# First attention of an eight-layer kernel: the order of extra product and transposes in TensorE's units

## The reference, cut to what matters

```
q = rope((x @ Wq.T + bq)) * key_weight / sqrt(64)   # 32 heads of 64
k = rope(x @ Wk.T + bk)                             # 8 key heads of 64
v = x @ Wv.T + bv                                   # 8 value heads of 64
p = softmax(causal(q @ k.T))                        # per head, 256 x 256
x = x + (concat(p @ v) @ Wo.T + bo)
```

## Time and profile before

| | us |
|---|---|
| median of 3 runs | 1513.32 |
| lowest and highest | 1510.92 and 1513.45 |
| profiled execution, own time | 1510.35 |
| its span | 1508.6 |
| TensorE busy | 1165.2 (77%) |
| VectorE busy | 987.3 (65%) |
| ScalarE busy | 599.3 (40%) |
| GpSimd busy | 582.0 (39%) |

### The profile page before, as it was taken

The page is one execution under the profiler, slowest core; times in us unless marked ns, Lnnn a source line. Parts: engine busy times, 40 slices in busy tenths (PEclk is TensorE's granted clock), DMA queues, the critical chain, the costliest instruction groups (busy, mean ns, idle before and its releaser), DMA issues. The chain is left out here.

```text
span 1508.6 us, 18582 instructions
## 1 busy us (share of the span) xinstructions
PE 1165.2 (77%) x5824; PEld 849.9 (56%) x5824; DVE 987.3 (65%) x1940; ACT 599.3 (40%) x1413; POOL 582.0 (39%) x462
## 2 busy tenths in 40 slices
PE   0167899989787868995769982999999956069988
PEld 0044556555556646431468872888888832048876
DVE  7757777777658866671513444788888858963345
ACT  3145555565644435315114331433333324133333
POOL 4346565565505540441042234434434401504420
PEclk9988999999989989998669995999999977579999
DMA  1121121210111101200423422010000000001101
GB/s 64 45 56 50 29 64 42 61 43 19 29 32 32 42 7 46 80 0 0 179 76 133 149 94 88 30 42 29 28 28 28 4 12 23 0 23 49 56 21 59
DMA packets 28955, 71.31 MB, mean 47 GB/s; under 512 B 4960, under 2 KB 14688, under 8 KB 26080
## 3 DMA queue, kind: packets, MB, share of 16 engines
q1 hardware_dynamic: 26320, 65.34, 14.0%
q0 software_dynamic: 1536, 4.20, 1.0%
q10 hardware_dynamic: 1040, 1.05, 0.2%
HBM read 55.89 MB, written 4.19 MB: 40 GB/s over the span
## 5 line engine op out<-in xcount | busy, mean ns | idle before, releaser
L176 POOL TENSOR_TENSOR sums<-scans 128x512 f32<-128x512 f32 x64 | 82.7, 1292 | 325.9 <-DVE scans L159 169.7
L510 ACT ACTIVATE probs<-ps_s,stats 128x256 f32<-128x256 f32 (+1 forms) x256 | 104.1, 418 | 101.6 <-DVE stats L577 101.6
L671 PE MATMUL ps_p<-xin,wkvq 128*128 128x512 f32 x148 | 75.9, 638 | 71.1 <-DMA wkvq<-w_l0a_dram 71.1
L456 POOL TENSOR_TENSOR probs<-probs,stats 128x512 f32<-128x512 f32 x64 | 67.4, 1053 | 127.1 <-DVE stats L583 127.1
L196 DVE RECIPROCAL sums<-sums 128x256 f32<-128x256 f32 x64 | 112.1, 1752 | 1.9
L577 DVE CUSTOM_DVE_ANT_0 ps_s<-ps_s,mask 128x256 f32<-128x256 f32 (+1 forms) x256 | 83.5, 387 | 22.8 <-PE ps_s L697 22.7
L181 POOL TENSOR_TENSOR sums<-sums,terms 128x512 f32<-128x512 f32 x64 | 87.1, 1361 | 4.4
L894 POOL TENSOR_TENSOR L3hid<-L3hid,L3sig 128x1024 f32 (+1 forms) x17 | 45.3, 2669 | 88.8 <-ACT L3sig L957 49.9
L671 PEld LDWEIGHTS ps_p<-xin,wkvq 128*128 128x128 f32 x148 | 27.1, 203 | 91.4 <-DMA wkvq<-w_l0a_dram 68.8
L1787 PE MATMUL K_ps_kvp<-K_wqkv_hi,K_xin_hi 128*128 128x256 f32 x256 | 74.8, 292 | 0.0
L1787 PE MATMUL K_ps_kvp<-K_wqkv_lo,K_xin_hi 128*128 128x256 f32 x256 | 72.3, 282 | 0.0
(11 more groups left out here) (375 smaller groups left out, 3577.8 us busy)
## 6 DMA issues: line engine op xcount, KB each, us to landing
E_fc<-l_fc_dram SPq DMA_DIRECT2D x16, 1024.0 KB, 6.6
qswap<-qraw SPq DMA_DIRECT2D x64, 128.0 KB, 2.3
K_wqkv<-l_wqkv_dram SPq DMA_DIRECT2D x16, 384.0 KB, 3.1
L3wgu<-L_w_dram SPq DMA_DIRECT2D x17, 256.0 KB, 2.6
L0wgu<-L_w_dram SPq DMA_DIRECT2D x14, 256.0 KB, 2.6
wkvq<-w_l0a_dram SPq DMA_DIRECT2D x4, 768.0 KB, 4.4
L3wdn<-L_w_dram SPq DMA_DIRECT2D x17, 128.0 KB, 2.0
wo<-w_l0a_dram SPq DMA_DIRECT2D x4, 512.0 KB, 3.6
```

Source lines behind the costliest of these rows:

```text
L176: pstep.mark(pool.tensor_tensor(sums[:, k, :, :], scans[:, k, :, 0, :], scans[:, k, :, 1, :], ALU.add))
L456: pool.tensor_tensor(p1, p1, rs[:, 0:2].unsqueeze(2).to_broadcast([P, 2, T]), ALU.mult)
L510: ins = act.activation(dst[:, i % 2, :], src[:, i % 2, :], ACT.Exp, bias=stats[:, g % 4, 4 + i:5 + i], scale=-1.0, accum_out=stats[:, g % ...
L671: ins = pe.matmul(ps[:, :], w[:, k, :], xin[:, k, h * HALF:(h + 1) * HALF], start=(k == 0), stop=(k == CH - 1))
```

## The change

In TensorE's loop over the units, the transposes of unit g-2 move behind the extra product. The order score, transposes, extra, values becomes score, extra, transposes, values. In a unit without an extra nothing changes.

```diff
@@ -732,13 +732,13 @@
                     for u in range(NU):
                         g = c * NU + u
                         score(g)
-                        if g >= 2:
-                            turn(g - 2)
                         if slot_item(c, u):
                             item(*slot_item(c, u))
                         if c and u in WO_SLOT:
                             pe.wait_ge(*emptied[c - 1, WO_SLOT[u]])
                             out_part(c - 1, WO_SLOT[u], ps_p[:, :])
+                        if g >= 2:
+                            turn(g - 2)
                         if g >= 3:
                             weigh(g - 3)
                 turn(ALL - 2)
```

## The result

| | before | after |
|---|---|---|
| median, us | 1512.13 (11 runs) | 1517.62 (11 runs) |
| lowest and highest | 1510.92 and 1513.45 | 1512.05 and 1519.22 |
| profiled execution, own time | 1510.35 | 1519.12 |
| its first scores to the start of the last output product | 86.63 to 411.88: 325.25 | 86.94 to 417.32: 330.38 |

The change made the kernel slower by 5.5 us by the medians; the ratio to the kernel before is 1.003, with an interval of 1.0019 to 1.0042. The forecast was 1509.8 with a range of 1503.5 to 1516.5. It grew by 5.1 us.

A forecast was written before the change was run, and what follows sets the result against it. TensorE was taken as busiest (77% of the span), with about 6.2 us of its own waits per full pair to win. Terms -3.9 - 0.4 + 0.5 + 0.3 = -3.5 us gave 1509.8 us, range 1503.5 to 1516.5.

The forecast's parts named there:

- the 5.1: Pair 0: VectorE's maxima of unit 7, the last projection of q, its swap and the next weights' load come 5.1 us earlier.
- 1.2 us go back: Pair 0, unit 9: transposes now stand behind the projection that waits for the load, giving back 1.2 us, leaving -3.9.
- VectorE late by 0.3: Last pair: extras up to unit 8, then VectorE late by 0.3 us; +0.3 in all.
- Where an output product follows (...), its extra 1.7 us on TensorE let the others catch up, so I count no loss there: Units 4, 5, 8 and 1 of later pairs: the output product's extra 1.7 us absorbs lateness; no loss counted.
- 1.0 us of new waiting: Later pairs, after units 3, 7, 10 and 15: VectorE's later copy makes the extra after next wait 1.0 us for its bank.
- The new wait for unit 13's values: The first output product waits for ScalarE's value evacuation of unit 13: 0.65 us taken, between nothing and 1.3.
- Nothing is added or removed.: Whole change: 52 extras start up to 0.65 us earlier, transposes later by the extra's length; no added work counted.
- wins 0.4 between unit 10 and the next unit 0: Later pairs: TensorE wins 0.4 us there, as the 2.63 us wait in the k rotation chain shrinks to about 2.3.
- rival 2: Later pairs, units 3, 7, 10, 15: VectorE's late copy sets the pace, 1.0 us each; about 6 slower, 1519; chance 0.15.
- Rival 1: Later pairs: the extras swallow all TensorE waits ahead of the transposes too; 21 us gained, 1492; chance 0.05.
- Rival 3: No change: only 2.5 us of pair 0's gain survives, later pairs give back 1 to 3; 1513; chance 0.20.
- Rival 4: Units 10 to 13, three pairs: VectorE's rotations separate from GpSimd's product, 2.0 us each, 6 more gained; 1504; chance 0.12.

The follow-up runs named there:

- number 4: Changed kernel with the old order (transposes ahead of the extra) in units 1, 9 and 15 of each pair: 1509.19 us, ratio 0.9979 to the kernel before.
- again: The changed kernel run once more, unedited, for a second profile: 1518.47 us in one run, stretch 329.87 us.
- the copy last: Changed kernel with VectorE's copy of the transposes moved behind its unit's side work: 1508.1 us, ratio 0.9974 to the kernel before.
- numbers 4 and 5: Number 5: changed kernel with the old order only in unit 9 of each pair: 1513.52 us, ratio 1.0011 to the kernel before.

## Why the prediction was wrong

**Pair 0, the mechanism held, the end of it did not.** Unit 2's projection went into the wait (92.36, wait 3.80 left of 5.71), and the maxima of unit 3 came 2.7 us earlier (101.37, with the first scores 0.30 later; 2.5 was forecast). At unit 9 the scores were 4.4 us earlier in the first profile and 6.7 in the second, around the 5.1. What failed is the term "1.2 us go back": unit 10 was left with -2.2 and -3.4, so 2.2 and 3.3 went back. The transposes behind the projection took 1.16 and 1.42, about as forecast (0.65 to 1.3). What the sum lacked is that the end of the load wait did not follow the scores: it came 3.4 and 5.3 us earlier where they came 4.4 and 6.7, because the last of the four transfers of the swap, issued ahead of the load in SyncE's queue, took 1.62 and 2.10 us to issue in place of 0.59. What held it there isn't known. In the profile of number 4 it took 0.60 and all of the gain stayed (-6.7 at unit 9, -6.9 at unit 10); with only unit 9 in the old order 1.5 went back.

**Later pairs: this is where the forecast failed.** Its terms against the table, in us:

| part | forecast | changed kernel | again |
|---|---|---|---|
| pair 0, unit 10 to pair 1, unit 0 | -0.4 | +0.6 | +0.6 |
| pairs 1 and 2, unit 0 to unit 10, each | +0.65 | +1.5 and +1.7 | +1.2 and +1.2 |
| pairs 1 and 2, unit 10 to the next unit 0, each | -0.4 | +1.0 and -0.7 | +1.7 and 0.0 |
| last pair | +0.3 | +3.2 | +3.2 |
| sum | +0.4 | +7.2 | +7.9 |

**The largest miss is the last pair.** "VectorE late by 0.3" stood for it. The runs showed 2.7 us between units 9 and 15 in both profiles: TensorE's wait for GpSimd 3.43 in place of 2.42, and behind it a granted clock of 0.56 (391.2 to 397.9) where the kernel before has 1.00. With the copy last nothing is lost there.

**The step "Where an output product follows (...), its extra 1.7 us on TensorE let the others catch up, so I count no loss there" failed at unit 15.** It was right after units 3 and 7, where the differences stand still. It was applied to unit 15, which has an output product only one unit further on: its projection waited 1.43, 2.27 and 2.27 us in pairs 0 to 2 (1.21, 2.65 and 1.45 in the second profile), and in pair 1 it cost 3.1 and 3.5 us together with what the clock took. The wait for the evacuation of q was known, as "1.0 us of new waiting"; that here nothing behind it makes it good was left out. The 1.0 itself took 4.1 us for a unit, which is 4.18 by the prediction's own pieces and 4.22 in the new order; with 4.22 it is 0.8. The order isn't all of it: the chain of the next q's rotation runs as before in pair 1 (243.70, before 243.69), TensorE comes to it earlier and waits, and two kernels with the old order in this unit, where the transposes waited 2.91 and 3.10 for that chain, lost 3.7 and 3.9 there.

**The new wait for unit 13's values was in the sum at 0.65.** The timeline shows 1.12 in pair 2, and in the first profile the scores of unit 2 are 1.2 us later against unit 1 in each pair. It is near the upper bound of 1.3 and gives 0.75 back one unit later, where a wait for GpSimd is now covered.

**A term was missing:** the load wait of unit 9 in pairs 1 and 2. Before, there was none, as the transposes came first; the changed kernel shows 0.84 and 1.17 us ahead of the projection. By unit 11 it costs 0.6 per pair, and the old order in unit 9 costs the same, as shown under numbers 4 and 5.

**Another was put at nothing:** "Nothing is added or removed." A unit with an extra takes 0.045 us more in the new order, an estimated 1.8 us over pairs 1 to 3.

**What came as a gain.** The forecast's "wins 0.4 between unit 10 and the next unit 0" was too small at unit 13, which gave 1.9 back in pair 1. Most of that is the clock: before, the transposes and the projection behind the wait of 2.63 took 1.00 and 3.19 from start to start, and in the changed kernel the projection took 1.89 and the transposes 0.75. Unit 15 took it again.

**What the profile would show.** The load wait over 4 us, the waits moving to the projections and VectorE's waiting for the transposes (52.9 us in 38 waits) came as written. Pair 1 lasted 84.5 (84.9 in the second profile), past the 84 that stood as a sign of rival 2, and pair 2 83.1 (83.2), between the 82.6 of right and the 84 of wrong.

**The rivals.** Rival 2 gave the sign and nearly the time (1519, with 0.15). Of its places unit 15 waited, and 3, 7 and 10 lost little or nothing. The wait for unit 13's values that it counted in full came nearly so. The copy last on the changed kernel and number 4 take away different things, the copy's place in VectorE's order and three waits on TensorE, and either alone brings the kernel below the one before. That the late copy makes the path late at those units, and only there loses time, agrees with both, but is argued and not shown by a run of its own. Rival 1 fell: the waits at the projections took the place of those it saw swallowed. Rival 3's giving back in the later pairs came, but went on past zero. Rival 4's event came where it was expected, in unit 11 of pair 1, and paid next to nothing. The rotation of k took 1.23 in place of 3.19, but the quotient behind it on VectorE then ran beside GpSimd's product and took 2.45 in place of 0.43, so the next maxima started at 234.69 before and at 234.68 after, with the first scores 0.30 later (before, then after):

```profile
234.35 0.43 DVE L199 TENSOR_TENSOR mod<-sums 128x256 f32<-128x256 f32 x1
```

```profile
231.04 1.23 DVE L556 TENSOR_TENSOR t<-kswap,rope 128x1024 f32<-128x1024 f32 x1 [0.27 <-DMA kswap<-kraw]
...
232.30 2.45 DVE L199 TENSOR_TENSOR mod<-sums 128x256 f32<-128x256 f32 x1
```

In unit 11 of pair 2 and in unit 8 of pairs 1 to 3 it went the other way, 1.91 before and 2.98 after, and 1.65 before and 2.21 after. These overlaps agree with the Trainium skill, SBUF — State Buffer, section "Who interferes with whom", by which the instruction that starts second waits for the first. Alone the rotation took 1.22. With 0.58, 1.13, 1.18, 1.50 and 2.10 us of GpSimd's product left at its start it took 1.65, 2.21, 2.26, 2.58 and 3.19, which is longer by what was left less 0.13 to 0.15 each time. In the last pair's wait the other side is second: GpSimd's multiplication of 0.61 took 1.59 behind VectorE's addition.

**Open.** The time outside the stretch is 1188.7 us in the changed kernel's profile and 1185.1 in that of before, which is 3.6 of the 8.8 us between the two profiled executions. It is 1188.6 in the second profile of the changed kernel, 1188.1 with the new order in pair 0 alone, 1185.45 with it in the later pairs alone and 1185.1 in number 4. The later stages have the same code in all of them, and what decides between these values wasn't settled. In the changed kernel TensorE is busy 873.3 us behind the stretch with the same instructions, 868.8 before. Nor was it tried to hold the clock up after the 2.27 us waits, so how much of the loss is waiting and how much the clock isn't separated. That the three exceptions together remove the loss is measured; of their parts only unit 1's (0.8 to 1.3 us per pair in both profiles, nothing with the old order there) stands out clearly, and no run has it alone.

## What to carry to other kernels

Where every unit of a pipeline is written alike, a reordering is a separate question for each unit: what does the moved work wait for there (a load, its bank, an evacuation), and does it now hold work that was ready. Here three exceptions among 16 units turned a loss of 0.3% into a gain of 0.2%. And an order on one engine fixes by when another engine's copy is due: the same move of VectorE's copy brought 8.5 us with one order on TensorE and cost 30 with the other, so the two are to be changed together. An engine that comes early to a chain that it does not set only waits there longer, and may pay for the wait once more in clock: 5.9 us of lead became 2.1 in one unit.

## What the runs showed of the hardware that was not expected

The granted clock after waits of the same length differs, within one execution and between executions. In the changed kernel the projection of unit 15 took 2.93 us after a wait of 2.27 in pair 1, and 1.98 after a wait of 2.27 in pair 2:

```profile
334.06 1.98 PE L671 MATMUL ps_p<-xin,wkvq 128*128 128x512 f32 x4 [2.27 <-ACT qraw L499]
```

With only unit 9 in the old order, unit 15 of pair 1 has the same wait of 2.27 and took 1.98 too.

The changed kernel's runs spread over 7.2 us (1512.05 to 1519.22), and those of the kernel before over 2.5 in one set and over 4.5 to 8.3 in the others. The scores of one unit moved by 2.3 us between profiles with the same program up to there, so one profile of such a kernel can't size a cost below some 2 us.
